# The causal mask of the diagonal score blocks: from two small TensorE products to one VectorE addition

## Chip, cores, metric

The kernel runs on one core of a Trainium2 chip. The metric is the time of one execution on the device in microseconds (us); of several runs the median is given.

## What is computed

The input x has 8 sequences of 512 rows of 128 numbers, in float32. Three layers follow one another: half a mixture-of-experts feed-forward of the normalised rows (32 experts of 64 hidden columns, the 6 best taken within 2 of 4 groups, 16 anchors of 32, one shared expert), then causal attention, then the same feed-forward again. The change touches the attention alone:

```
q, k, v = layernorm(x) @ Wq, Wk, Wv            # 16 heads of 64
scores  = q k^T / 8 + (0 where key <= query, else -inf)
attn    = softmax(scores)                       # over the keys
x       = x + layernorm(x) + (attn v) @ Wo
```

## The kernel before

All engines are programmed by hand. Each has one list of instructions that it works off in order, and semaphores tie the lists together: `pe.wait_ge(s["q_lo"], n + 1)` holds everything that follows it on that engine until VectorE has counted q_lo up to n + 1. There is no scheduler.

The rows are in chunks of 512, one sequence each, so the attention has 8 batches b. Each has 8 slots p, one for a pair of heads, 64 slots in all; n = 8b + p numbers the pairs. float32 products are made of three float32r products, of a high and a low part of each operand: ScalarE takes the high part out of PSUM (`part_hi`: k_hi, q_hi), VectorE the rest (`part_lo`: k_lo, q_lo).

A slot is a software pipeline over four pairs. TensorE's list for slot n (`attn_slot`, L572) is, in this order:

1. `probT` of pair n-1, group 1: 16 transposes of probabilities into PSUM. Its wait, `second_ready`, asks for pT_dve 2n-1, which is VectorE's copy of group 0 of pair n-1, the last copy in the slot before.
2. `scores` of pair n+1, unit 0 (query block 3, 512 keys), then unit 1 (query block 2, 384 keys). In unit 1 the function `third_ready` waits, just ahead of the last products, for the two copies of group 1.
3. `probT` of pair n-1, group 2, then the k projection of pair n+2, a v projection, the output projection of pair n-2, and the q projection of pair n+2, which shares its bank with k and so waits for k_lo.
4. `scores` of pair n+1, unit 2 (query blocks 1 and 0, 256 columns of two banks each), which waits for the exponentials of unit 0 to free the banks.
5. `probT` of pair n, group 0 (16 transposes), then `attend` of pair n-1, 16 products, which wait for q_lo.

A unit writes both heads of the pair, i = 0 and 1, into two PSUM banks. Its real products are L517. After them come four products at L527, which add the mask to the diagonal block: the identity times the mask, both in bf16, in two halves of 64 rows (k = 0, 1), once for each head. They cover 128 columns of each head in units 0 and 1, and 256 in unit 2. Their operands lie in the tile `half`, loaded as float32 and cast by VectorE at L1231 in the first chunk of the first feed-forward.

VectorE's list for a slot (`attn_slot`, L1308) is: copy of group 1 of pair n-1 (`pT_copy`), reciprocal of the row sums (`row_rec`), `row_max` of units 0 and 1 of pair n+1, k_lo, q_lo, `row_max` of unit 2 (two reductions), copy of group 0 of pair n. Some slots have more: p = 1 and 2 normalise rows of the next batch, p = 2 adds the output of the batch before and takes statistics, p = 3 ends these, p = 4 (batches 0 to 6) makes the low part of the next batch's rows ahead of k_lo and has its k projection after the v projection; two slots at the end of batch 6 and the start of batch 7 are shaped like p = 4 for the second feed-forward. Batch 7 carries pieces of routing.

ScalarE's list is: context copy of pair n-2 (`ctx_copy`), its halves of groups 1 and 2, k_hi, the two exponentials of unit 0 (`exp`), the copy of v, q_hi, the two exponentials of unit 1, the four of unit 2. In the slots p = 1 of batches 1 to 7 it also copies the output ahead of q_hi. GpSimd multiplies the probabilities with the reciprocals.

Of the kernel before, what the change touches and what calls it, by code (L numbers as in the profile page):

```python
# [31 lines left out]
P = 128  # L32
# [25 lines left out]
def constants():  # L58

    ident = np.eye(P, dtype=np.float32)  # L60
    mask = np.where(np.arange(P)[None, :] > np.arange(P)[:, None], NEG, 0.0)
    halves = [np.tile(m[i * DK:(i + 1) * DK], (2, 1)) for m in (ident, mask) for i in (0, 1)]
    halves = halves[0:2] + [halves[2], halves[2], halves[3], halves[3]]
    iota = np.broadcast_to(np.arange(E, dtype=np.float32)[None, :], (P, E))
    tie = np.broadcast_to((np.arange(G)[None, :] < np.arange(G)[:, None]), (P, TB, G, G))
    small = np.concatenate([ident, iota, tie.reshape(P, -1), *halves], 1)
    return small.astype(np.float32)


def build(nc, x_in, wg_in, wu_in, wd_in, gate_in, bias_in, wq_in, wk_in, wv_in, wo_in,  # L70
# [6 lines left out]
    with ctx:  # L77
        def sb(name, shape, dt=F32):
            return ctx.enter_context(nc.sbuf_tensor(name, shape, dt))
# [6 lines left out]
        def sem(name):  # L86
# [4 lines left out]
        ident = small[:, 0:P]  # L91
        iota = small[:, P:P + E]
        tie = small[:, P + E:].rearrange("p (t a b) -> p t a b", t=TB, a=G)
        half = sb("half", [P, 6 * P], BF16)
        gate_w = sb("gate_w", [P, E])
        bias = sb("bias", [P, E])
        wg = [sb(f"wg_{n}", [P, HC], F32R) for n in ("hi", "lo")]
# [13 lines left out]
        NZ = 5  # L111
        z = [work[:, i * CH:(i + 1) * CH] for i in range(5, 5 + NZ)]
        spread = work[:, 10 * CH:].rearrange("p (k c) -> p k c", k=NSPREAD)
        half_f32 = work[:, 5 * CH:5 * CH + 6 * P]
        prob = work[:, 0:4 * PW].rearrange("p (r i c) -> p r i c", r=2, i=2)
        values = [work[:, 10 * CH:].rearrange("p (t d) -> p t d", t=TB),
                  sb("values", [P, TB, CH])[:, :, :]]
# [52 lines left out]
        psT, psA, psO = pairs[2], bank[6], bank[7]  # L170


        names = """small_loaded gate_loaded half_loaded half_ready attn_w_loaded
            stat_dve stat_act stat_rows stat_bn rsqrt
            xn_ready xT_ps xT_sb logits_ps sigmoid_done route cwT_ps cwT_sb xT_hi xT_lo
            one_plus gate_up_ps cw_stored silu_done gated_done z_done z_hi z_lo down_ps
            y_evac yT_ps x_added
            aw_hi aw_lo
            a_xn a_xT_ps a_xT_hi a_xT_lo a_xres
            q_ps k_ps v_ps q_hi q_lo k_hi k_lo v_sb s_ps max_done exp_done rec_done norm_done  # L180
            pT_ps pT_act pT_dve ctx_ps ctx_sb out_ps outT_sb outT_ps out_added stored""".split()
        s = {n: sem("s_" + n) for n in names}
        x_loads = [sem(f"s_x_load{c}") for c in range(NC)]
# [72 lines left out]
        def ahead(b, p, d):  # L256

            return b + (p + d) // HP, (p + d) % HP
# [31 lines left out]
        def _(sp):  # L290
# [17 lines left out]
            sp.dma_start(bias[:, :], bias_in.partition_broadcast(P)).then_inc(s["gate_loaded"], 16)  # L308
            load_group(sp, 0)
            load_x(sp, 1)  # L310
            sp.dma_start(half_f32, small_in[:, SMALL:]).then_inc(s["half_loaded"], 16)
            load_group(sp, 1)
            load_down(sp, 0)
            load_down(sp, 1)
            for c in range(2, NC):
                load_x(sp, c)
            for k in range(2, W_GROUPS):
# [53 lines left out]
        def _(pe):  # L371
# [131 lines left out]
            def scores(b, p, u, first, transposes_ready=None):  # L503

                n = pair(b, p)
                if u == 0:
                    pe.wait_ge(s["q_lo"], n + 1)
                    pe.wait_ge(s["k_lo"], n + 1)
                if not (first and p == 0 and u < 2):
                    pe.wait_ge(s["exp_done"], 3 * n + (-1, 0, 1)[u])  # L510
                ps = score_banks(p, u)
                blocks = ([(3, 0, CH)], [(2, 0, 3 * P)], [(1, 0, 2 * P), (0, 2 * P, 2 * P)])[u]
                for qb, o, w in blocks:
                    for k, (a, c) in enumerate(((0, 0), (0, 1), (1, 0))):
                        for i in (0, 1):
                            r = slice(i * DK, (i + 1) * DK)
                            pe.matmul(ps[:, i, o:o + w], qk[0][a][r, p % 2, qb * P:(qb + 1) * P],  # L517
                                      qk[1][c][r, p % 2, 0:w], start=qb != 0 and k == 0, stop=False,
                                      skip_group_check=True)

                o, w = ((3 * P, P), (2 * P, P), (P, 2 * P))[u]
                for k in (0, 1):
                    if k == 1 and transposes_ready is not None:
                        transposes_ready()
                    for i in (0, 1):
                        r = slice(i * DK, (i + 1) * DK)
                        m = pe.matmul(ps[:, i, o:o + w], half[r, k * P:(k + 1) * P],  # L527
                                      half[r, 2 * (k + 1) * P:2 * (k + 1) * P + w], start=False,
                                      stop=k == 1, skip_group_check=True)
                m.then_inc(s["s_ps"], 1)  # L530

            def probT(b, p, g):
# [405 lines left out]
        def _(dve):  # L938
# [240 lines left out]
            def ffn_chunk(g, g0, first, last):  # L1179
# [6 lines left out]
                for j in range(HT):  # L1186
                    if j == 0 and not last and not after_attention:
                        dve.wait_ge(s["xT_ps"], g + 1)
                        normalise(g + 1 - g0, "xn_ready")
                    if setup and j >= 3:  # L1190
                        dve.wait_ge(s["z_done"], tiles(g, j - 3))
                    dve.wait_ge(s["silu_done"], tiles(g, j))
                    if j < HT - 1:
                        tt(gated[j % 3], psU[j % 3], silu[j % 2], ALU.mult) \  # L1194
                            .then_inc(s["gated_done"], 1)
                    else:
                        tt(gated[j % 3][MI:, :], psG[j % 3][MI:, :], silu[j % 2][MI:, :], ALU.mult) \
                            .then_inc(s["gated_done"], 1)
                    if j == 9 and not first:
                        add_y(g - 1, g0)  # L1200
                    if j == XT + 3 and not last:
                        xT_low(g + 1)
                    if j in ROUTING and not last:
                        ROUTING[j](g + 1)
                    if after_attention and j == 18:
                        rows_stats(NC - 1)
                    if after_attention and j == 19:
                        rows_mean(NC - 1, 3 * NC - 1)
                    if j == at_stats and measure:
                        dve.wait_ge(s["x_added"], g)  # L1210
                        rows_stats(g - 1)
                    if j == at_mean and measure:
                        rows_mean(g - 1, middle_stats(g - 1))
                    if g < NC - 2 and j == at_input_stats:
                        dve.wait_ge(x_loads[g + 2], 16)
                        rows_stats(g + 2)
                    if g < NC - 2 and j == at_input_stats + 1:
                        rows_mean(g + 2, input_stats(g + 2))
                    if 0 < g < NC - 2 and j == 18:
                        finish_std(g + 2)  # L1220
                    if before_attention and j == 15:
                        finish_std(STD_MIDDLE)
                    if before_attention and j == 16:
                        a_rows(0, True, range(TB))
                    if before_attention and j == 17:
                        a_residual(0)
                    if setup and j == 2:
                        split_lo(1, 0)
                        split_lo(1, 1)
                        dve.wait_ge(s["half_loaded"], 16)  # L1230
                        nc.vector.tensor_copy(half[:, :], half_f32).then_inc(s["half_ready"], 1)  # L1231
                        dve.wait_ge(s["half_ready"], 1)
                    for k in range(setup_scaled(j - 1), setup_scaled(j)) if setup else (j,):
                        scale(g, k, first)
                if setup:
# [30 lines left out]
            def part_lo(b, p, which, early, special=False):  # L1266
# [9 lines left out]
                else:  # L1276
                    tt(lo, ps, f32(hi), ALU.subtract).then_inc(s["k_lo"], 1)

            def row_max(b, p, u):
                n = pair(b, p)  # L1280
                dve.wait_ge(s["s_ps"], 3 * n + u + 1)
                ps = score_banks(p, u)
                for qb, o in (((3, 0),), ((2, 0),), ((1, 0), (0, 2 * P)))[u]:
                    m = nc.vector.tensor_reduce(nmax[:, p % 2, :, qb], ps[:, :, o:o + (qb + 1) * P],  # L1284
# [23 lines left out]
            def attn_slot(b, p, first, last):  # L1308
# [6 lines left out]
                if p == 2 and not first:  # L1315
                    add_out(b - 1)
                if have_s:
                    row_max(*ahead(b, p, 1), 0)
                    row_max(*ahead(b, p, 1), 1)
                if next_rows(b, p):  # L1320
                    a_xT_low(b + 1, psA)
                if ffn_rows(b, p):
                    xT_low(NC)
                if have_q:
                    part_lo(*ahead(b, p, 2), 1, False, special_slot(b, p))
                if p == 2 and not first:
                    dve.wait_ge(s["out_added"], b)
                    rows_stats(b - 1)
                if p == 3 and not first:
                    rows_mean(b - 1, b - 1 + 2 * NC)  # L1330
                if have_q:
                    part_lo(*ahead(b, p, 2), 0, False)
                if have_s:
                    row_max(*ahead(b, p, 1), 2)
                if pair(b, p) == NC * HP - 1:
                    route_onehot(NC)
# [22 lines left out]
                        piece(NC)  # L1359

            def attention():
                row_max(0, 0, 0)
                row_max(0, 0, 1)
                add_y(NC - 1, 0)
                part_lo(0, 1, 1, True)
                row_max(0, 0, 2)
                part_lo(0, 1, 0, True)
                for p in range(HP):
# [117 lines left out]
```

## Time and profile before

| | |
|---|---|
| median of 3 runs | 1465.37 us (1463.87 to 1465.82) |
| the profiled execution | 1465.29 us, its span 1463.5 us |
| TensorE busy | 1426.8 us, 97% |
| VectorE busy | 1081.9 us, 74% |
| ScalarE busy | 805.5 us, 55% |
| GpSimd busy | 286.3 us, 20% |
| first feed-forward | about 0 to 418 us of the span |
| attention | about 418 to 1054 us |
| second feed-forward | to the end |

The span is the time from the first instruction to the last on the chip. Busy time counts instructions that overlap once. An engine that is busy for 97% of the span leaves little for others to wait on, but a product that is counted as busy may still stream slower than it could, and the share is an average over three stages.

### The profile page before, as it was taken

Reading aid. Unit: us, or ns where it says so; the run is one execution under the profiler, and the core shown is the slowest. Engines: PE = TensorE matmul, PEld = TensorE weight load, DVE = VectorE, ACT = ScalarE, POOL = GpSimd, SP = SyncE. Lnnn points to the kernel's source line nnn. Section 1 sums busy time; section 2 is a strip of 40 time slices with the busy share of each in tenths; the row PEclk is TensorE's granted clock in tenths of the full one; section 3 lists DMA queues with packets and bytes.
Section 4 is the critical chain, followed back from the end, with each engine's and each line's share of the span. In section 5 each row is a group of like instructions: output and inputs, shape, how many; then the busy total and the mean of one; then the engine's idle time right before and its main releaser. Section 6 shows DMA issues by size and latency. Waiting matters only on the chain.

```text
span 1463.5 us, 27264 instructions
## 1 busy us (share of the span) xinstructions
PE 1426.8 (97%) x9616; PEld 951.9 (65%) x9616; DVE 1081.9 (74%) x2451; ACT 805.5 (55%) x1911; POOL 286.3 (20%) x585
## 2 busy tenths in 40 slices
PE   5999999999979999999999999999899999999998
PEld 4666666666656666666666666666566666666665
DVE  8888888888667676776767677767767877787775
ACT  4344344433457777777787777777644233323332
POOL 1000000000214344344444434434400000000000
PEclk9999999999999999999999999999999999999999
DMA  6543333333300000000000000000033433333332
GB/s 229 161 131 110 111 102 117 106 116 98 114 22 2 1 2 2 2 2 2 1 2 2 2 2 2 2 2 2 2 110 108 121 116 113 110 119 121 111 118 86
DMA packets 59024, 98.06 MB, mean 67 GB/s; under 512 B 6160, under 2 KB 15504, under 8 KB 58896
## 3 DMA queue, kind: packets, MB, share of 16 engines
q1 hardware_dynamic: 58896, 96.38, 21.1%
q8 instruction: 77, 1.26, 0.4%
q14 instruction: 51, 0.42, 0.1%
HBM read 92.68 MB, written 3.67 MB: 66 GB/s over the span
## 4 chain that ended last, share of the span: by engine, by line
PE 90%; DVE 4%; ACT 3%; issue 1%; POOL 0%; DMA 0%; SPq 0%; POOLq 0%; ACTq 0%; DVEq 0%
PE banks L416 19%; PE banks L199 14%; PE banks L201 13%; PE banks L200 13%; PE banks L552 10%; PE banks L517 9%; PE banks L538 6%; PE banks L565 3%; PE banks L527 2%; PE banks L375 2%; ACT work L843 1%; PE banks L387 1%; DVE q_lo L1273 1%; DVE work L1194 1%; POOL work L1428 0%
## 5 line engine op out<-in xcount | busy, mean ns | idle before, releaser
L787 ACT ACTIVATE work<-banks 128x512 f32<-128x512 f32 x320 | 190.9, 597 | 444.8 <-PE banks L201 440.8
L416 PE MATMUL banks<-work,wd 128*128 128x512 f32 x672 | 342.1, 592 | 0.3 <-DVE work L1168 0.2
L1194 DVE TENSOR_TENSOR work<-banks,work 128x512 f32<-128x512 f32 x320 | 220.8, 690 | 145.7 <-ACT work L787 141.3
L843 ACT ACTIVATE work<-banks,nmax 128x512 f32<-128x512 f32 (+3 forms) x512 | 263.7, 527 | 39.1 <-DVE nmax L1284 39.1
L1428 POOL TENSOR_SCALAR work<-work,rrec 128x512 f32<-128x512 f32 (+3 forms) x512 | 262.7, 542 | 0.0
L199 PE MATMUL banks<-xT_hi,wg_hi 128*128 128x512 f32 x336 | 248.4, 739 | 0.7 <-DVE wu_lo L1159 0.6
L1168 DVE TENSOR_TENSOR work<-work 128x512 f32<-128x512 f32 x320 | 225.3, 704 | 7.4 <-DMA work<-cw_rows 3.3
L1284 DVE TENSOR_REDUCE nmax<-banks 128x2 f32<-128x1024 f32 (+3 forms) x256 | 198.9, 818 | 9.9 <-PE banks L527 5.5
L1299 DVE COPY stage<-banks 128x1024 f32<-128x1024 f32 (+1 forms) x128 | 122.0, 953 | 59.0 <-PE banks L538 58.8
L416 PEld LDWEIGHTS banks<-work,wd 128*128 128x128 f32 x672 | 126.5, 189 | 33.7 <-issue 2.4
L201 PE MATMUL banks<-xT_hi,wg_lo 128*128 128x512 f32 x336 | 133.7, 398 | 0.0
L200 PE MATMUL banks<-xT_lo,wg_hi 128*128 128x512 f32 x336 | 133.5, 397 | 0.0
L199 PE MATMUL banks<-xT_hi,wu_hi 128*128 128x512 f32 x320 | 127.2, 397 | 0.0
L200 PE MATMUL banks<-xT_lo,wu_hi 128*128 128x512 f32 x320 | 127.1, 397 | 0.0
L201 PE MATMUL banks<-xT_hi,wu_lo 128*128 128x512 f32 x320 | 127.0, 397 | 0.0
L854 ACT ACTIVATE stage<-banks 128x512 f32<-128x512 f32 x128 | 76.5, 598 | 86.7 <-PE banks L538 84.6
L538 PE MATMUL banks<-small,work 64*128 64x64 f32 x2560 | 114.6, 225 | 4.3 <-DVE stage L1299 2.7
L538 PEld LDWEIGHTS banks<-small,work 64*128 64x128 f32 x2560 | 98.2, 138 | 17.6 <-issue 16.0
L1273 DVE SCALAR_TENSOR_TENSOR q_lo<-banks,q_hi 128x512 fp32r<-128x512 f32 x64 | 44.3, 692 | 87.0 <-ACT q_hi L821 87.0
L199 PEld LDWEIGHTS banks<-xT_hi,wg_hi 128*128 128x128 f32 x336 | 64.3, 191 | 67.9 <-issue 65.3
L200 PEld LDWEIGHTS banks<-xT_lo,wg_hi 128*128 128x128 f32 x336 | 64.4, 192 | 65.6 <-issue 65.3
L843 ACT ACTIVATION_READ_ACCUMULATOR work<-banks,nmax 128x1 f32 x512 | 105.4, 206 | 0.0
(135 smaller groups left out, 2191.6 us busy)
## 6 DMA issues: line engine op xcount, KB each, us to landing
work<-cw_rows SPq DMA_DIRECT2D x320, 256.0 KB, 3.1
x<-in_x SPq DMA_DIRECT2D x8, 256.0 KB, 6.6
out_rows<-x SPq DMA_DIRECT2D x8, 256.0 KB, 2.2
cw_rows<-cwT SPq DMA_DIRECT2D x16, 96.0 KB, 1.9
stage<-in_w_gate SPq DMA_DIRECT2D x3, 448.0 KB, 4.9
wd<-in_w_down SPq DMA_DIRECT2D x3, 448.0 KB, 7.7
stage<-in_w_up SPq DMA_DIRECT2D x2, 448.0 KB, 6.5
stage<-in_wq SPq DMA_DIRECT2D x1, 512.0 KB, 4.0
```

The lines of the kernel that those rows point to most:

```text
L199: pe.matmul(o, w[0], m[0], start=start, stop=False, skip_group_check=True)
L200: pe.matmul(o, w[0], m[1], start=False, stop=False, skip_group_check=True)
L201: return pe.matmul(o, w[1], m[0], start=False, stop=stop, skip_group_check=True)
L416: pe.matmul(psY, wd[:, j * P:(j + 1) * P], z[part_slot(j)], start=j == 0, stop=j == HT - 1, skip_group_check=True).then_inc(s["down_ps"], 1)
L538: m = pe.transpose(psT[:, h, k * DK:(k + 1) * DK], prob[r, p % 2, i, o:o + P], ident[r, h * DK:(h + 1) * DK])
L552: m = pe.matmul(psA[i * DK:(i + 1) * DK, kb * P:], values[p // TB][:, kb, p % TB * P + i * DK:p % TB * P + (i + 1) * DK], pT[:, p % 2, o:o ...
L787: nc.scalar.activation(silu[j % 2], psG[j % 3], ACT.Silu) \
L843: m = nc.scalar.activation(prob[:, p % 2, i, o:o + w], ps[:, i, so:so + w], ACT.Exp, bias=nmax[:, p % 2, i, qb:qb + 1], accum_out=rsum[:, ...
L1168: tt(z[part_slot(j)], gated[j % 3], spread[:, j % NSPREAD, :], ALU.mult) \
L1194: tt(gated[j % 3], psU[j % 3], silu[j % 2], ALU.mult) \
L1284: m = nc.vector.tensor_reduce(nmax[:, p % 2, :, qb], ps[:, :, o:o + (qb + 1) * P], AX.X, ALU.max, negate=True)
L1428: nc.gpsimd.tensor_scalar(t, t, rrec[:, par, i, qb:qb + 1], 1.0, ALU.mult, ALU.mult) \
```

## The change

VectorE gets the mask as a float32 tile of 128 x 128 and adds it in PSUM, in place, to the diagonal block of each unit, for both heads in one instruction, and the row maximum waits for that. An instruction covers 256 elements in each partition in units 0 and 1, and 512 in unit 2. TensorE's four bf16 products of each unit go. The wait that stood between them (`transposes_ready`) now stands ahead of the last pair of the real products. On VectorE the row maximum of unit 1 moves behind k_lo; the addition of unit 1 stays where that maximum was. The load of 384 KB of bf16 operands as float32, with its cast, goes, and a load of 64 KB takes its place, two issues later on the same queue.

```diff
-        half = sb("half", [P, 6 * P], BF16)
+        mask = sb("mask", [P, P])
@@ SyncE
-            sp.dma_start(half_f32, small_in[:, SMALL:]).then_inc(s["half_loaded"], 16)
             load_group(sp, 1)
             load_down(sp, 0)
             load_down(sp, 1)
+            sp.dma_start(mask[:, :], small_in[:, SMALL:]).then_inc(s["mask_loaded"], 16)
@@ TensorE, scores()
                 for qb, o, w in blocks:
+                    final = qb in (3, 2, 0)
                     for k, (a, c) in enumerate(((0, 0), (0, 1), (1, 0))):
+                        if k == 2 and final and transposes_ready is not None:
+                            transposes_ready()
                         for i in (0, 1):
                             r = slice(i * DK, (i + 1) * DK)
-                            pe.matmul(ps[:, i, o:o + w], qk[0][a][r, p % 2, qb * P:(qb + 1) * P],
-                                      qk[1][c][r, p % 2, 0:w], start=qb != 0 and k == 0, stop=False,
-                                      skip_group_check=True)
-
-                o, w = ((3 * P, P), (2 * P, P), (P, 2 * P))[u]
-                for k in (0, 1):
-                    if k == 1 and transposes_ready is not None:
-                        transposes_ready()
-                    for i in (0, 1):
-                        r = slice(i * DK, (i + 1) * DK)
-                        m = pe.matmul(ps[:, i, o:o + w], half[r, k * P:(k + 1) * P],
-                                      half[r, 2 * (k + 1) * P:2 * (k + 1) * P + w], start=False,
-                                      stop=k == 1, skip_group_check=True)
+                            m = pe.matmul(ps[:, i, o:o + w], qk[0][a][r, p % 2, qb * P:(qb + 1) * P],
+                                          qk[1][c][r, p % 2, 0:w], start=qb != 0 and k == 0,
+                                          stop=final and k == 2, skip_group_check=True)
                 m.then_inc(s["s_ps"], 1)
@@ VectorE, first chunk
-                        dve.wait_ge(s["half_loaded"], 16)
-                        nc.vector.tensor_copy(half[:, :], half_f32).then_inc(s["half_ready"], 1)
-                        dve.wait_ge(s["half_ready"], 1)
@@ VectorE, attention
+            def mask_scores(b, p, u):
+                n = pair(b, p)
+                dve.wait_ge(s["s_ps"], 3 * n + u + 1)
+                if n == 0 and u == 0:
+                    dve.wait_ge(s["mask_loaded"], 16)
+                o, w = ((3 * P, P), (2 * P, P), (P, 2 * P))[u]
+                ps = score_banks(p, u)[:, :, o:o + w].rearrange("p i (b c) -> p i b c", c=P)
+                tt(ps, ps, mask[:, :].unsqueeze(1).unsqueeze(1).broadcast_to([P, 2, w // P, P]), ALU.add) \
+                    .then_inc(s["masked"], 1)
             def row_max(b, p, u):
-                dve.wait_ge(s["s_ps"], 3 * n + u + 1)
+                dve.wait_ge(s["masked"], 3 * n + u + 1)
@@ attn_slot of VectorE
+                    mask_scores(*ahead(b, p, 1), 0)
                     row_max(*ahead(b, p, 1), 0)
-                    row_max(*ahead(b, p, 1), 1)
+                    mask_scores(*ahead(b, p, 1), 1)
 ...
                 if have_q:
                     part_lo(*ahead(b, p, 2), 1, False, special_slot(b, p))
+                if have_s:
+                    row_max(*ahead(b, p, 1), 1)
 ...
                     part_lo(*ahead(b, p, 2), 0, False)
                 if have_s:
+                    mask_scores(*ahead(b, p, 1), 2)
                     row_max(*ahead(b, p, 1), 2)
```

## Rows read from the trace of the kernel before

**Rows 1.** The page: busy time of each engine.

```profile
PE 1426.8 (97%) x9616; PEld 951.9 (65%) x9616; DVE 1081.9 (74%) x2451; ACT 805.5 (55%) x1911; POOL 286.3 (20%) x585
```

**Rows 2.** The page: the chain that ended last, share of the span by line.

```profile
PE banks L416 19%; PE banks L199 14%; PE banks L201 13%; PE banks L200 13%; PE banks L552 10%; PE banks L517 9%; PE banks L538 6%; PE banks L565 3%; PE banks L527 2%; PE banks L375 2%; ACT work L843 1%; PE banks L387 1%; DVE q_lo L1273 1%; 
```

**Rows 3.** The chain in order of time, one slot: start us, us, what.

```profile
668.64 0.64 PE banks L538 x16
669.28 0.75 PE banks L517 x6
670.16 0.58 PE banks L517 x6
670.87 0.25 PE banks L538 x8
...
675.29 0.23 PE banks L527 x4
...
678.33 0.64 PE banks L538 x16
```

**Rows 4.** Timeline, that slot, VectorE: start us, us, instruction, idle before.

```profile
669.33 0.69 DVE L1299 COPY stage<-banks 128x512 f32<-128x512 f32 x1 [1.20 <-PE banks L538]
670.20 2.09 DVE L1284 TENSOR_REDUCE nmax<-banks 128x2 f32<-128x1024 f32 x2
672.67 0.69 DVE L1277 TENSOR_TENSOR k_lo<-banks,k_hi 128x512 fp32r<-128x512 f32 x1 [0.38 <-ACT k_hi L821]
675.05 0.69 DVE L1273 SCALAR_TENSOR_TENSOR q_lo<-banks,q_hi 128x512 fp32r<-128x512 f32 x1 [1.69 <-ACT q_hi L821]
675.66 1.01 DVE L1284 TENSOR_REDUCE nmax<-banks 128x2 f32<-128x512 f32 x2
676.59 1.21 DVE L1299 COPY stage<-banks 128x1024 f32<-128x1024 f32 x1
```

**Rows 5.** Timeline, that slot, TensorE and ScalarE.

```profile
673.42 0.19 PEld L199 LDWEIGHTS banks<-xT_hi,aw_hi 128*128 128x128 f32 x1 [0.62 <-DVE k_lo L1277]
674.42 0.60 ACT L821 ACTIVATE q_hi<-banks 128x512 fp32r<-128x512 f32 x1
675.95 2.38 PE L552 MATMUL banks<-stage,values 128*64 128x512 f32 x16
676.71 0.47 ACT L843 ACTIVATE work<-banks,nmax 128x256 f32<-128x256 f32 x1 [0.57 <-DVE nmax L1284]
678.26 0.71 PE L538 MATMUL banks<-small,work 64*128 64x64 f32 x16
678.38 0.60 ACT L865 ACTIVATE ctx_sum<-banks 128x512 f32<-128x512 f32 x1
```

**Rows 6.** Groups by line and shape, 420 to 1020 us: busy, mean ns, idle.

```profile
L1284 DVE TENSOR_REDUCE nmax<-banks 128x2 f32<-128x512 f32 x60 | 40.9, 682 | 0.0
L1284 DVE TENSOR_REDUCE nmax<-banks 128x2 f32<-128x256 f32 x60 | 25.0, 417 | 0.0
```

**Rows 7.** Timeline, routing of the first chunk, VectorE.

```profile
14.74 0.18 DVE L1034 TENSOR_TENSOR t<-t 128x32 f32<-128x32 f32 x1
14.85 0.18 DVE L1035 TENSOR_TENSOR t<-t 128x32 f32<-128x32 f32 x1
15.06 0.19 DVE L1037 TENSOR_TENSOR t<-t,t 128x32 f32<-128x32 f32 x1
```

**Rows 8.** Timeline, slots p = 1 and p = 4 of one batch, VectorE.

```profile
685.18 0.69 DVE L1273 SCALAR_TENSOR_TENSOR q_lo<-banks,q_hi 128x512 fp32r<-128x512 f32 x1 [2.11 <-ACT q_hi L821]
...
714.34 0.69 DVE L1277 TENSOR_TENSOR k_lo<-banks,k_hi 128x512 fp32r<-128x512 f32 x1 [1.62 <-ACT k_hi L821]
715.35 0.69 DVE L1273 SCALAR_TENSOR_TENSOR q_lo<-banks,q_hi 128x512 fp32r<-128x512 f32 x1 [0.31 <-ACT q_hi L821]
```

**Rows 9.** Timeline, VectorE behind the cast, and at the first scores.

```profile
29.79 0.69 DVE L1168 TENSOR_TENSOR work<-work 128x512 f32<-128x512 f32 x1 [0.23 <-DMA work<-cw_rows]
...
418.07 2.09 DVE L1284 TENSOR_REDUCE nmax<-banks 128x2 f32<-128x1024 f32 x2 [1.19 <-PE banks L527]
```

More of the change, by code:

```diff
@@ L61, in constants @@
     mask = np.where(np.arange(P)[None, :] > np.arange(P)[:, None], NEG, 0.0)
-    halves = [np.tile(m[i * DK:(i + 1) * DK], (2, 1)) for m in (ident, mask) for i in (0, 1)]
-    halves = halves[0:2] + [halves[2], halves[2], halves[3], halves[3]]
     iota = np.broadcast_to(np.arange(E, dtype=np.float32)[None, :], (P, E))
     tie = np.broadcast_to((np.arange(G)[None, :] < np.arange(G)[:, None]), (P, TB, G, G))
-    small = np.concatenate([ident, iota, tie.reshape(P, -1), *halves], 1)
+    small = np.concatenate([ident, iota, tie.reshape(P, -1), mask], 1)
     return small.astype(np.float32)
@@ L113, in build @@
         spread = work[:, 10 * CH:].rearrange("p (k c) -> p k c", k=NSPREAD)
-        half_f32 = work[:, 5 * CH:5 * CH + 6 * P]
         prob = work[:, 0:4 * PW].rearrange("p (r i c) -> p r i c", r=2, i=2)
@@ L170, in build @@
         psT, psA, psO = pairs[2], bank[6], bank[7]
-        names = """small_loaded gate_loaded half_loaded half_ready attn_w_loaded
+        names = """small_loaded gate_loaded mask_loaded attn_w_loaded
             stat_dve stat_act stat_rows stat_bn rsqrt
@@ L179, in build @@
             a_xn a_xT_ps a_xT_hi a_xT_lo a_xres
-            q_ps k_ps v_ps q_hi q_lo k_hi k_lo v_sb s_ps max_done exp_done rec_done norm_done
+            q_ps k_ps v_ps q_hi q_lo k_hi k_lo v_sb s_ps masked max_done exp_done rec_done norm_done
             pT_ps pT_act pT_dve ctx_ps ctx_sb out_ps outT_sb outT_ps out_added stored""".split()
@@ L1361, in attention @@
             def attention():
+                mask_scores(0, 0, 0)
                 row_max(0, 0, 0)
+                mask_scores(0, 0, 1)
                 row_max(0, 0, 1)
@@ L1365, in attention @@
                 part_lo(0, 1, 1, True)
+                mask_scores(0, 0, 2)
                 row_max(0, 0, 2)
```

## The prediction

> **What bounds the kernel now.** I read the page first. TensorE is busy 97% of the span and VectorE 74% [rows 1], and the chain that ended last is TensorE almost throughout, with the mask products at 2% [rows 2]. So the first reading is: the products that go are on the chain, and VectorE has time for the additions. Shares don't settle it, though, so I then laid one ordinary slot out in order of time, once by the chain [rows 3] and once with all engines [rows 4, 5]. The reader is to see three things there.
>
> First, the slot lasts 678.33 - 668.64 = 9.69 us, and TensorE streams through it. In the list of the chain the mask products of units 0 and 1 are gaps: 669.28 + 0.75 = 670.03 to 670.16 is 0.13 us, 670.16 + 0.58 = 670.74 to 670.87 is again 0.13, and unit 2's are a row of their own, 0.23 [rows 3]. Together 0.49 us a slot, 64 x 0.49 = 31 us of the span, which is the 2% of [rows 2].
>
> Second, VectorE's idle time lies where it waits for others: 1.20 us ahead of the copy of group 1, 0.38 ahead of k_lo, 1.69 ahead of q_lo, 3.3 us in 9.69. Behind q_lo it has none until the slot is over: q_lo at 675.05, row maxima of unit 2 at 675.66, copy of group 0 from 676.59 to 677.80 [rows 4].
>
> Third, TensorE's next slot begins at 678.26 [rows 5] with transposes that overwrite what this copy reads (`second_ready`). From VectorE's end to TensorE's start such a wait takes 673.42 - (672.67 + 0.69) = 0.06 us [rows 4, 5]. The copy would have let TensorE start at 677.80 + 0.06 = 677.86. The slack of this second chain is 0.40 us, and it is what the change spends.
>
> **The change part by part.** I count from T, the start of a slot's first transposes: T = 678.26 - 9.69 = 668.57.
>
> *TensorE, units 0 and 1.* The products that go save 0.13 + 0.13. A part of these gaps may be a pause between kinds of product that stays in another form; a pair of 512 columns takes 0.23, so four of 128 should stream in half that, 0.12. I take 0.25 for the two units, bounds 0.2 and 0.26. Everything down to q_hi follows TensorE, provided that VectorE's part above is hidden, which I check next: q_hi starts at T + 5.85 [rows 5] and would start at T + 5.60.
>
> *VectorE, units 0 and 1.* The trace has no addition that writes PSUM. The nearest rows are the subtraction of 512 elements from PSUM and SBUF, 0.69 us [rows 4], and reductions of 512 and 256 elements, 0.68 and 0.42 [rows 6]. I take 0.42 and 0.69; nothing of that kind is below the 0.42, and a write into PSUM could cost some 0.1 more. The addition is followed by a wait of the engine for its own result. Three small operations show what that costs: without a wait the next starts 14.85 - 14.74 = 0.11 after the last, with one 15.06 - 14.85 = 0.21, for the same 0.18 of duration [rows 7]. So a waiting successor starts at duration plus 0.03, a free one at duration less 0.08. Addition 0 can start when unit 0 is through, at about T + 1.5; the maximum of unit 0 follows at 1.95 to 3.18, addition 1 at 3.1 to 3.5. k_lo before stands at T + 4.10 and must move to T + 3.85, since the q projection starts right at its end; VectorE is free 0.3 us earlier. The moved maximum of unit 1, with 0.95 us, fits the idle 1.69 between k_lo and q_lo. Cost of these: nothing, covered by VectorE's own idle time. Without that cover it would be 0.42 for each addition.
>
> *VectorE, unit 2.* Here nothing covers. q_lo at T + 6.48 moves to T + 6.23 and its successor to T + 6.84. Before, that was the maximum of unit 2; now it is the addition of 512 elements, and the maximum comes 0.69 + 0.03 = 0.72 later. The scores themselves are ready in time, so the 0.23 that TensorE saves in unit 2 is worth nothing. The copy of group 0 ends at 677.80 - 668.57 = T + 9.23, less 0.25, plus 0.72: T + 9.70, and TensorE may go on at T + 9.76. Before it went on at T + 9.69. **An ordinary slot thus becomes 0.07 us longer**, where a slot bound by TensorE alone would be 0.49 shorter. Bounds: 0.2 saved and an addition 0.1 dearer give +0.22; a wait that costs nothing gives -0.04.
>
> *The rule.* The skill weighs the wait otherwise. The Trainium skill, VectorE: DVE Perf Modes, section The DRAIN you can't avoid, says that chained operations cost the same with a semaphore after each as with one at the end, and advises to keep the number of operations down, not the semaphores. By that the maximum would come 0.61 behind the addition, and the slot would be 0.04 shorter than before; the rows above speak against it, with 0.21 against 0.11. Its other half, fewer operations, speaks against the change.
>
> *TensorE's moved wait.* In unit 1 `third_ready` now stands ahead of the last real pair, about 0.1 us earlier within the unit. It asks for ScalarE's copy of group 1, which stands behind the exponentials of unit 2 and the context copy. These start 0.04 us behind the maximum [rows 4, 5], now at T + 8.6; the context copy follows 678.38 - 676.71 = 1.67 us later at the most, about T' + 0.5 with T' the next slot's start, and the copy of group 1 ends at about T' + 1.6. The loading of weights behind the wait stood at T' + 1.55. It is just met: 0 to 0.1 us.
>
> *Slots with more in them.* p = 1, seven of them: ScalarE holds q_hi back, VectorE idles 2.11 us and q_lo is at 685.18 [rows 8], so TensorE waits for q_lo and sets the end of the slot some 0.6 us later than the copy would; the 0.25 is kept: 7 x -0.25 = -1.8. p = 4, seven, and two like it: k_lo comes at 714.34 and q_lo 1.01 behind it [rows 8]. The moved maximum must fit between: k_lo, 0.61, maximum, 0.87, q_lo is 1.48, so q_lo is 0.47 late, on top of the 0.07: 9 x 0.54 = +4.9. p = 2, seven: addition of the output ahead of unit 0 and statistics between k_lo and q_lo take up the cover; I take 0.2 each, +1.4, bounds 0.07 and 0.5. The remaining 64 - 23 = 41 slots x 0.07 = +2.9. In the first two slots and ahead of them TensorE already waits for VectorE: the first maximum idles until TensorE's unit 0 is through [rows 9], so an addition of 0.45 less 0.13 is on the path there, and one of 0.72 twice; I take +1.5. The end of batch 7, with routing behind the copy of group 0, I take as +0.5.
>
> *Loads.* The cast goes, but VectorE idles 0.23 us for a load right behind it [rows 9], so the next multiplication stays where it is: 0. The mask is needed 380 us later: 0. The feed-forwards are unchanged.
>
> Sum: -1.8 + 4.9 + 1.4 + 2.9 + 1.5 + 0.5 = +9.4. The profiled execution took 1465.29 us and becomes 1474.7; the median before is 0.1 higher, so I say **1474.7 us**.
>
> **The rivals.**
>
> *A: TensorE stays the bound (faster).* If TensorE can start its slot when its own work is done, the change gives 64 x -0.49 = -31: 1434 us. For it: 97% against 74%. Against it: the copy of group 0 would have to end by T + 9.14, 0.56 earlier than I find. It decides where addition and wait together take below 0.16 us in unit 2, or where the copy is not what releases the transposes. A mixture, with half of this, would be 1450.
>
> *B: the wait is free.* If the successor starts 0.61 behind the addition (this is what the rule above claims), 0.11 less in 57 slots is -6: 1468.5, slower by 0.2%, at the edge of what can be measured; with the full 0.26 saved, 1467. Against it: 0.21 against 0.11 in [rows 7].
>
> *C: ScalarE's late copy catches TensorE, or PSUM is dear.* If `third_ready` is met 0.15 to 0.2 us late, or the addition of unit 2 costs that much more than a subtraction that writes SBUF, 57 x 0.17 = +10: 1485. For it: 0.05 us of margin in my own reckoning. Against it: the wait holds a weight load that runs ahead of its product by about as much.
>
> **How the numbers follow.** About 0.2%, 3 us, is what a measurement of this kernel tells from no change. My forecast has a chance of 0.52, its own range 1468.5 to 1481; A 0.14; B 0.12; C 0.17; something else, 0.05, half to each side. The range leaves out A, the far end of C and the like, and keeps B and half of the unknown: 1460 to 1487. Faster than 1462.4: A and the half, with the lowest part of B, 0.18. Within 3 us: most of B and the low edge of the forecast, 0.12. Slower: 0.70.
>
> **What would show it.** The chain that ended last should no longer run on TensorE alone in ordinary slots: q_lo, the addition of unit 2, the maxima, the copy L1299, then the transposes L538, with TensorE idle about 0.5 us ahead of these. The additions should read 0.42 and 0.69 us, the maximum of unit 2 should start 0.72 behind the addition, and a slot should last 9.76. In p = 4 q_lo should be late behind the moved maximum. VectorE's idle time ahead of q_lo should fall from 1.69 to about 0.8. VectorE's busy time should rise by 64 x (0.42 + 0.42 + 0.69) = 98 us. Wrong would be: no wait of TensorE for L1299 (A); a wait of TensorE for the copy of ScalarE in unit 1 (C); a granted clock below the present one, which I don't price.

## The result and the profile after

The changed kernel takes 1481.49 us (median of 4 runs, 1481.23 to 1483.76), the kernel before, on the same chip, 1465.59. The ratio is 1.0111, with a 95% interval of 1.0096 to 1.0126: 14 to 18.5 us slower. The profiled execution has a span of 1479.9 us, 16.4 more than before. All of it arises in the attention: VectorE's last copy of group 1 starts at 1078.65 us, before at 1062.27.

The page's busy times and the chain that ended last, as in [rows 1] and [rows 2]:

```profile
PE 1404.6 (95%) x8848; PEld 947.1 (64%) x8848; DVE 1170.0 (79%) x2642; ACT 798.3 (54%) x1911; POOL 286.1 (19%) x585
...
PE 65%; DVE 17%; ACT 10%; issue 7%; POOL 0%; DMA 0%; SPq 0%; DVEq 0%; POOLq 0%; ACTq 0%
PE banks L413 19%; PE banks L196 12%; PE banks L198 11%; PE banks L197 11%; PE banks L517 5%; ACT work L833 5%; DVE stage L1296 4%; PE banks L528 4%; DVE nmax L1281 3%; DVE q_lo L1260 3%; DVE banks L1273 3%; ACT q_hi L811 2%; PE banks L372 
```

TensorE has 768 products and 22 us of busy time less, VectorE 88 us more, and the chain now passes through VectorE's q_lo (L1260), the addition (L1273), the maxima (L1281) and the copy (L1296). ScalarE's share of it is 10%, where it was 3%: in an ordinary slot the chain goes from k_hi through ScalarE's list (the exponentials of unit 0, the copy of v) to q_hi, and from there to q_lo. In the groups of the window 420 to 1020 us the row of the transposes names the new wait, 28.4 us for the copy L1296; before, all 2360 of them in the same window had idled 1.9 us. The rows, first TensorE, then the additions of both shapes:

```profile
L528 PE MATMUL banks<-small,work 64*128 64x64 f32 x2296 | 103.5, 224 | 28.4 <-DVE stage L1296 28.4
L1273 DVE TENSOR_TENSOR banks<-banks,mask 128x256 f32<-128x256 f32 x117 | 49.9, 427 | 3.4 <-PE banks L517 3.4
L1273 DVE TENSOR_TENSOR banks<-banks,mask 128x512 f32<-128x512 f32 x59 | 40.7, 690 | 0.0
```

One ordinary slot in the timeline, with the rows that answer to [rows 4] and [rows 5]. T, the start of the first transposes (the loading of their weights), is 666.90 here:

```profile
666.90 0.60 PEld L528 LDWEIGHTS banks<-small,work 64*128 64x128 f32 x16 [0.72 <-issue]
667.29 0.61 ACT L855 ACTIVATE ctx_sum<-banks 128x512 f32<-128x512 f32 x1
667.76 0.62 ACT L844 ACTIVATE stage<-banks 128x512 f32<-128x512 f32 x1
668.43 0.43 DVE L1273 TENSOR_TENSOR banks<-banks,mask 128x256 f32<-128x256 f32 x1
668.50 0.22 PEld L517 LDWEIGHTS banks<-k_hi,q_lo 64*128 64x128 f32 x2
668.78 0.44 PE L528 MATMUL banks<-small,work 64*128 64x64 f32 x8
668.90 1.23 DVE L1281 TENSOR_REDUCE nmax<-banks 128x2 f32<-128x1024 f32 x1
670.04 0.42 DVE L1273 TENSOR_TENSOR banks<-banks,mask 128x256 f32<-128x256 f32 x1
670.77 0.69 DVE L1264 TENSOR_TENSOR k_lo<-banks,k_hi 128x512 fp32r<-128x512 f32 x1 [0.31 <-ACT k_hi L811]
671.38 0.95 DVE L1281 TENSOR_REDUCE nmax<-banks 128x2 f32<-128x768 f32 x1
671.52 0.19 PEld L196 LDWEIGHTS banks<-xT_hi,aw_hi 128*128 128x128 f32 x1 [0.63 <-DVE k_lo L1264]
672.52 0.60 ACT L811 ACTIVATE q_hi<-banks 128x512 fp32r<-128x512 f32 x1
673.15 0.69 DVE L1260 SCALAR_TENSOR_TENSOR q_lo<-banks,q_hi 128x512 fp32r<-128x512 f32 x1 [0.82 <-ACT q_hi L811]
673.76 0.69 DVE L1273 TENSOR_TENSOR banks<-banks,mask 128x512 f32<-128x512 f32 x1
674.49 1.02 DVE L1281 TENSOR_REDUCE nmax<-banks 128x2 f32<-128x512 f32 x2
675.42 1.22 DVE L1296 COPY stage<-banks 128x1024 f32<-128x1024 f32 x1
676.75 0.61 PEld L528 LDWEIGHTS banks<-small,work 64*128 64x128 f32 x16 [0.72 <-issue]
676.78 0.68 PE L528 MATMUL banks<-small,work 64*128 64x64 f32 x15 [0.51 <-DVE stage L1296]
```

The slot lasts 676.75 - 666.90 = 9.85 us, against 9.69 before. The reader is to see that VectorE runs from 673.15 to 676.64 without a pause, and that TensorE waits 0.51 us for the last of these operations while it has nothing else to do. Above q_lo VectorE still has pauses: the additions of units 0 and 1 delay nobody.

### The profile page after: what moved, and what is told of

Same layout as the page of the kernel before. It is cut to its first block, busy times and chain, and to the rows that moved or that the text cites. A ratio compares the mean times of both kernels' runs of the same rounds, so it can differ in the third digit from the quotient of the medians.

```text
span 1479.9 us, 25920 instructions
## 1 busy us (share of the span) xinstructions
PE 1404.6 (95%) x8848; PEld 947.1 (64%) x8848; DVE 1170.0 (79%) x2642; ACT 798.3 (54%) x1911; POOL 286.1 (19%) x585
## 4 chain that ended last, share of the span: by engine, by line
PE 65%; DVE 17%; ACT 10%; issue 7%; POOL 0%; DMA 0%; SPq 0%; DVEq 0%; POOLq 0%; ACTq 0%
PE banks L413 19%; PE banks L196 12%; PE banks L198 11%; PE banks L197 11%; PE banks L517 5%; ACT work L833 5%; DVE stage L1296 4%; PE banks L528 4%; DVE nmax L1281 3%; DVE q_lo L1260 3%; DVE banks L1273 3%; ACT q_hi L811 2%; PE banks L372 2%; PE banks L542 1%; ACT work L819 1%
## 5 line engine op out<-in xcount | busy, mean ns | idle before, releaser
L1281 DVE TENSOR_REDUCE nmax<-banks 128x2 f32<-128x1024 f32 (+3 forms) x256 | 204.7, 821 | 4.5
L1296 DVE COPY stage<-banks 128x1024 f32<-128x1024 f32 (+1 forms) x128 | 122.0, 953 | 37.7 <-PE banks L528 37.5
L528 PEld LDWEIGHTS banks<-small,work 64*128 64x128 f32 x2560 | 106.7, 138 | 48.0 <-issue 46.9
L1273 DVE TENSOR_TENSOR banks<-banks,mask 128x256 f32<-128x256 f32 (+1 forms) x192 | 98.7, 514 | 5.7 <-PE banks L517 5.7
```

The source lines that it names most:

```text
L528: m = pe.transpose(psT[:, h, k * DK:(k + 1) * DK], prob[r, p % 2, i, o:o + P], ident[r, h * DK:(h + 1) * DK])
L1296: nc.vector.tensor_copy(*transposed(p, g, slice(0, 2 - g))).then_inc(s["pT_dve"], 1)
```

## The experiments

T-numbers below are us behind the slot's first transposes. The length of a slot is read from the starts of VectorE's copy of group 1 in successive slots.

**Unit 2's mask back on TensorE.** The changed kernel, with the four bf16 products for unit 2 alone. The excerpt does not show the rest: their operands are loaded and cast again, VectorE adds nothing in unit 2, and its maximum waits for TensorE.

```diff
-                    final = qb in (3, 2, 0)
+                    final = qb in (3, 2, 0) and u not in (2,)
 ...
+                if u in (2,):
+                    o, w = ((3 * P, P), (2 * P, P), (P, 2 * P))[u]
+                    for k in (0, 1):
+                        if k == 1 and transposes_ready is not None:
+                            transposes_ready()
+                        for i in (0, 1):
+                            r = slice(i * DK, (i + 1) * DK)
+                            m = pe.matmul(ps[:, i, o:o + w], half[r, k * P:(k + 1) * P],
+                                          half[r, 2 * (k + 1) * P:2 * (k + 1) * P + w], start=False,
+                                          stop=k == 1, skip_group_check=True)
```

> Units 0 and 1 get the mask from VectorE as in the changed kernel, unit 2 from TensorE's bf16 products as before. My theory: only the addition of unit 2 lies on the chain (q_lo, addition, maxima, copy of group 0, next transposes), the additions of units 0 and 1 are hidden. Then TensorE sets an ordinary slot again and it lasts 9.69 - 0.25 = 9.44 us; with p = 1 at -0.25 and p = 4 at about +0.1 (moved maximum ahead of q_lo) the time is about 12 us below before: 1453 us. Rival, VectorE as a whole is too full and each addition costs alike: the slot stays near 9.69 or above, 1466 to 1476 us.

Measured: 1452.65 us, ratio to before 0.9906 (0.9891 to 0.9921). An ordinary slot lasts 9.38 us. Its timeline, VectorE and TensorE:

```profile
658.88 0.69 DVE L1282 TENSOR_TENSOR k_lo<-banks,k_hi 128x512 fp32r<-128x512 f32 x1 [0.26 <-ACT k_hi L826]
...
661.87 1.01 DVE L1304 TENSOR_REDUCE nmax<-banks 128x2 f32<-128x512 f32 x2
662.15 2.37 PE L557 MATMUL banks<-stage,values 128*64 128x512 f32 x16
662.79 1.22 DVE L1319 COPY stage<-banks 128x1024 f32<-128x1024 f32 x1
664.46 0.71 PE L543 MATMUL banks<-small,work 64*128 64x64 f32 x16
```

The copy ends at 664.01 and TensorE takes its transposes at 664.46, when its own products are through: it is the bound again. Two additions a slot, 64 x 2 x 0.43 = 55 us of VectorE's time, cost nothing; taking them in place of TensorE's products gains 13 us. The rival, that each addition costs alike, is out.

**Only unit 2 on VectorE.** The complement: the products of units 0 and 1 stay, with the load and the cast, and the maximum of unit 1 stays in its old place.

```diff
-                    final = qb in (3, 2, 0)
+                    final = qb in (3, 2, 0) and u not in (0, 1)
 ...
+                if u in (0, 1):            # the four products, as above
 ...
             def mask_scores(b, p, u):
+                if u not in (2,):
+                    return
```

> The kernel before with one part of the change alone: unit 2 gets the mask from VectorE, units 0 and 1 from TensorE, the maximum of unit 1 stays in its old place. My theory: nothing is saved ahead of q_hi, and all of addition and wait, 0.73 us, goes onto the chain against a slack of 0.35 to 0.40: an ordinary slot lasts about 10.08 us, 57 slots x 0.39 = +22: 1487 us, so more than the whole change. Rival, each addition costs alike: a third of the change's +16, 1471 us.

Measured: 1493.0 us, ratio 1.0186 (1.0171 to 1.0202). The slot lasts 10.13 us:

```profile
661.31 0.69 DVE L1319 COPY stage<-banks 128x512 f32<-128x512 f32 x1 [0.89 <-PE banks L543]
...
667.06 0.69 DVE L1278 SCALAR_TENSOR_TENSOR q_lo<-banks,q_hi 128x512 fp32r<-128x512 f32 x1 [1.69 <-ACT q_hi L826]
667.67 0.69 DVE L1293 TENSOR_TENSOR banks<-banks,mask 128x512 f32<-128x512 f32 x1
668.39 1.02 DVE L1304 TENSOR_REDUCE nmax<-banks 128x2 f32<-128x512 f32 x2
669.33 1.21 DVE L1319 COPY stage<-banks 128x1024 f32<-128x1024 f32 x1
671.44 0.69 DVE L1319 COPY stage<-banks 128x512 f32<-128x512 f32 x1 [0.89 <-PE banks L543]
```

One third of the change costs more than all of it, and more than the 1487 us expected: the slot is 0.43 us longer where 0.39 was reckoned, and 4.6 us are lost in the first slots of batch 0, which the expectation did not price. The two parts have opposite signs: -13 us and +27 us, with sum +14, near the whole change's +16. VectorE's idle 1.69 ahead of q_lo is as long as before and helps nothing.

**No mask in unit 2.** The changed kernel, leaving out the mask of query blocks 1 and 0; all bf16 products are gone, as in the change.

```diff
             def mask_scores(b, p, u):
+                if u not in (0, 1):
+                    return
```

> The changed kernel, leaving out the mask of unit 2 (query blocks 0 and 1 see later keys of their own block). My theory: the chain through VectorE ends at T + 9.74 - 0.73 + 0.11 = 9.12, TensorE's own work at 9.69 - 0.49 = 9.20, so an ordinary slot lasts 9.2 us and all that TensorE saves comes out: about -23 us, 1442 us. Rival, something else than the addition of unit 2 holds the slots (ScalarE's late copy, the maximum of unit 1): at or above 1460 us.

Measured: 1444.9 us, ratio 0.9856 (0.9841 to 0.9871), 37 us below the changed kernel for one instruction a slot less, and its wait. An ordinary slot lasts 9.23 us. In its timeline q_lo ends at 658.69 and the first weights of `attend` are loaded 0.06 us later, after waiting for it:

```profile
658.00 0.69 DVE L1260 SCALAR_TENSOR_TENSOR q_lo<-banks,q_hi 128x512 fp32r<-128x512 f32 x1 [0.82 <-ACT q_hi L811]
658.08 0.66 PE L528 MATMUL banks<-small,work 64*128 64x64 f32 x16
...
658.75 0.20 PEld L542 LDWEIGHTS banks<-stage,values 128*64 128x64 f32 x4 [0.15 <-DVE q_lo L1260]
```

So even with that addition at no cost, unit 2's products would be worth only 9.38 - 9.23 = 0.15 of their 0.23 us, since q_lo is next in line.

**The addition of unit 2 in two.** Each maximum waits for its own addition only, so the first one has an instruction between itself and what it reads.

```diff
-                ps = score_banks(p, u)[:, :, o:o + w].rearrange("p i (b c) -> p i b c", c=P)
-                tt(ps, ps, mask[:, :].unsqueeze(1).unsqueeze(1).broadcast_to([P, 2, w // P, P]), ALU.add) \
-                    .then_inc(s["masked"], 1)
+                for o in ((3 * P,), (2 * P,), (P, 2 * P))[u]:
+                    ps = score_banks(p, u)[:, :, o:o + P]
+                    tt(ps, ps, mask[:, :].unsqueeze(1).broadcast_to([P, 2, P]), ALU.add) \
+                        .then_inc(s["masked"], 1)
 ...
+                    dve.wait_ge(s["masked"], 4 * n + u + h + 1)     # ahead of each maximum
```

> The changed kernel, the addition of unit 2 as two of 256 elements, each maximum waiting for its own one only. If a wait of VectorE for its own last result costs the 0.12 us that I took, the first maximum starts 0.34 + 0.34 = 0.68 behind the first addition, not 0.73, and the slot is 0.05 us shorter: -3 us against the changed kernel, 1478 us. If waits are free, the additional instruction only costs: 0.68 against 0.61, +4 us, 1485 us. If what costs is mainly the number of instructions, also 1485 us.

Measured: 1477.34 us, ratio 1.008 (1.0066 to 1.0094), against 1.0111 (1.0096 to 1.0126) of the changed kernel. The slot lasts 9.77 us, 0.08 less. The timeline:

```profile
662.18 0.69 DVE L1260 SCALAR_TENSOR_TENSOR q_lo<-banks,q_hi 128x512 fp32r<-128x512 f32 x1 [0.81 <-ACT q_hi L811]
662.79 0.75 DVE L1273 TENSOR_TENSOR banks<-banks,mask 128x256 f32<-128x256 f32 x2
663.45 1.01 DVE L1281 TENSOR_REDUCE nmax<-banks 128x2 f32<-128x512 f32 x2
```

The maxima start 0.66 behind the first addition, where one addition of the same 512 elements took 674.49 - 673.76 = 0.73. One instruction more is cheaper here than one wait for the engine's own last result. The two intervals lie just apart, and the slot lengths show the same sign and size: 57 x 0.08 = 4.6 us.

The changed kernel has the same comparison within one slot p = 2. There VectorE is late, so that k_lo follows the addition of unit 1 without a wait for it:

```profile
1025.45 0.42 DVE L1273 TENSOR_TENSOR banks<-banks,mask 128x256 f32<-128x256 f32 x1
1025.79 0.68 DVE L1264 TENSOR_TENSOR k_lo<-banks,k_hi 128x512 fp32r<-128x512 f32 x1
```

It starts 0.34 us behind the addition's start (0.33 or 0.34 in all seven such slots), where the maximum of unit 0, which waits for its addition, starts 668.90 - 668.43 = 0.47 behind it.

**The maximum of unit 1 back in the nine slots with a late k projection.**

```diff
                     mask_scores(*ahead(b, p, 1), 1)
+                    if special_slot(b, p):
+                        row_max(*ahead(b, p, 1), 1)
 ...
-                if have_s:
+                if have_s and not special_slot(b, p):
                     row_max(*ahead(b, p, 1), 1)
```

> The changed kernel with the maximum of unit 1 back in its old place in the nine slots that have their k projection late (p = 4 of batches 0 to 6 and two like it), and only there. My theory: there the moved maximum stands between k_lo and q_lo, which are only 1.0 us apart, and makes q_lo 0.47 us late: 9 x 0.47 = -4 us against the changed kernel, about 1477 us; p = 4 falls from 10.96 to about 10.5 us. Rival, q_lo has room there: no difference.

Measured: 1478.6 us, ratio 1.0082 (1.0068 to 1.0096). The interval touches that of the changed kernel, so the gain rests on the slots: p = 4 lasts 10.49 us, in the changed kernel 10.95. First that slot in the changed kernel, then here:

```profile
722.60 0.69 DVE L1264 TENSOR_TENSOR k_lo<-banks,k_hi 128x512 fp32r<-128x512 f32 x1 [1.62 <-ACT k_hi L811]
723.21 0.95 DVE L1281 TENSOR_REDUCE nmax<-banks 128x2 f32<-128x768 f32 x1
724.08 0.68 DVE L1260 SCALAR_TENSOR_TENSOR q_lo<-banks,q_hi 128x512 fp32r<-128x512 f32 x1
```

```profile
719.67 0.96 DVE L1281 TENSOR_REDUCE nmax<-banks 128x2 f32<-128x768 f32 x1
...
721.96 0.69 DVE L1264 TENSOR_TENSOR k_lo<-banks,k_hi 128x512 fp32r<-128x512 f32 x1 [0.73 <-ACT k_hi L811]
722.97 0.69 DVE L1260 SCALAR_TENSOR_TENSOR q_lo<-banks,q_hi 128x512 fp32r<-128x512 f32 x1 [0.32 <-ACT q_hi L811]
```

The distance from k_lo to q_lo falls from 1.48 to 1.01 us, what it was in [rows 8]: the 0.47 of the forecast. The seven slots p = 4 gain 3.2 us together, and the two like them, of 11.44 and 11.31 us, another 1.3.

**The maximum of unit 1 back in all slots.** The same edit without the condition.

> The changed kernel with the maximum of unit 1 back in its old place in all slots. My theory: it ends at about T + 4.4, k_lo starts at T + 4.4 rather than at 3.87, the q projection and all behind it are 0.45 to 0.5 us late: an ordinary slot lasts about 10.3 us, +22 for 46 slots, -4 for the nine: 1499 us. Rival, the place of this maximum doesn't matter: 1481 us.

Measured: 1506.9 us, ratio 1.0281 (1.0265 to 1.0296). The ordinary slot lasts 10.43 us. k_lo follows the maximum without a pause and starts at T + 4.47 (T is 665.70 here), where the changed kernel has T + 3.87:

```profile
668.84 0.42 DVE L1273 TENSOR_TENSOR banks<-banks,mask 128x256 f32<-128x256 f32 x1
669.29 0.96 DVE L1281 TENSOR_REDUCE nmax<-banks 128x2 f32<-128x768 f32 x1
670.17 0.68 DVE L1264 TENSOR_TENSOR k_lo<-banks,k_hi 128x512 fp32r<-128x512 f32 x1
```

The 0.60 that k_lo is late comes back as 0.58 of the slot. So the additions of units 0 and 1 are free only because the maximum was moved with them: the cover is what VectorE idles ahead of k_lo in the changed kernel, 0.31 us. The time is 8 us above the 1499 expected. The ordinary slot was put 0.13 too short, and the seven slots p = 2 last 10.95 us in place of 9.95, 7 us together, for which nothing had been reckoned.

**Both findings together.** Unit 2's mask on TensorE, and the maximum of unit 1 early in the nine slots.

> Unit 2's mask on TensorE, units 0 and 1 on VectorE, and the maximum of unit 1 in its old place in the nine slots with the late k projection. My theory: as the run with unit 2 on TensorE, 1452.7 us, less up to 9 x 0.3 = 2.7 us (that slot lasted 9.68 us there, against 9.38 of an ordinary one): 1450 us, faster than the kernel before by 1%. Rival, those slots are held by TensorE's own extra work, 0.60 us: 1452.7 us.

Measured: 1448.05 us (1447.41 to 1449.08), ratio 0.9879 (0.9864 to 0.9894): 18 us faster than the kernel before and 33 us faster than the changed one. The slot p = 4 lasts 10.03 us, with 10.31 without this last edit (the expectation's 9.68 is not its length by the copies of group 1), and the nine slots together are 3.0 us shorter, where 2.7 was expected. What the last edit does to the whole time is not clear of noise: the intervals of this run and of the one with unit 2 on TensorE overlap.

## Why the prediction was right, point by point

The direction, the mechanism and its place were as forecast: slower, because the addition of unit 2 and the wait behind it outgrow the 0.40 us of slack of VectorE's second chain. The three runs that take the parts of the change by themselves show it. The measured time lies in the upper half of the range, 0.5 us above the likeliest case's own range; the shift was 16 us where the forecast had 9. The size was thus too small by 7 us, and nearly every term that missed missed to the same side.

*TensorE's saving ahead of q_hi.* Forecast 0.25; q_hi started at T + 5.62 instead of 5.85, so 0.23. In the run with unit 2 on TensorE k_lo stands at T + 3.80 instead of 4.10: 0.30 is there to be had. The changed kernel loses 0.07 of it at the moved wait of unit 1, behind which the weights of the second transposes are loaded at T + 1.73 here and at T + 1.66 there (T is 655.08 there). First the changed kernel, then that run:

```profile
668.63 0.45 PEld L528 LDWEIGHTS banks<-small,work 64*128 64x128 f32 x8
```

```profile
656.74 0.44 PEld L543 LDWEIGHTS banks<-small,work 64*128 64x128 f32 x8
```

ScalarE's context copy, which stands ahead of the copy that this wait asks for, is at T + 0.39 here and T + 0.12 there, and the last pair of unit 1 takes 397 ns here in the mean and 344 there. This is the mechanism of rival C, at a small size and within the 0 to 0.1 of the forecast. It is read from timelines and was not tried by itself.

*Additions.* Forecast 0.42 and 0.69, measured 0.427 and 0.690. An addition that reads and writes PSUM costs what the subtraction into SBUF costs, so the dear branch of C is out. These additions alone read 98.7 us, forecast 98; VectorE's busy time, which counts overlaps once, rose by 88. Its idle time ahead of q_lo fell to 0.82, forecast 0.8. The maximum starts 0.73 behind the addition, forecast 0.72.

*The rule on semaphores.* The Trainium skill, VectorE: DVE Perf Modes, section The DRAIN you can't avoid, has the semaphores within a chain of copies as free. Rival B was built on the same claim, and for these operations it is refuted: 0.73 with the wait, against 0.61 for the free successor of q_lo (673.15 to 673.76), 0.47 against 0.34 behind an addition of 256 elements, and the run with two additions got faster by putting an instruction in the place of the wait. So the advice on the number of operations, which that page gives under Rules for kernel authors, did not hold for this pair either.

*End of the chain.* The copy ends at T + 9.74, forecast 9.70. From there the loading of weights starts after 0.11 us, where I had taken 0.06 from k_lo. Slot 9.85 against 9.76; 0.16 longer than before and not 0.07. The right price stood in the trace of the kernel before, in the one slot in which TensorE did wait for this copy:

```profile
437.02 1.21 DVE L1299 COPY stage<-banks 128x1024 f32<-128x1024 f32 x1
438.35 0.60 PEld L538 LDWEIGHTS banks<-small,work 64*128 64x128 f32 x16 [2.03 <-issue]
```

438.35 - (437.02 + 1.21) = 0.12 us: a wait is best priced from a row of the same kind, even if there is only one.

*The sum by its terms*, from the copies of group 1 in both traces. The first term that was mis-sized is the ordinary slot: 34 of them (without the first four and the last three) cost 34 x 0.16 = 5.4, forecast 2.4. The seven p = 1 came out at 10.19 to 10.31 instead of 10.51 to 10.57, together -1.9 (forecast -1.8). The seven p = 2 at 9.95 instead of 9.70, +1.7 (forecast 1.4). The seven p = 4 at 10.95 instead of 10.33, +4.3 (forecast 3.8, of which 0.47 each was shown by putting the maximum back). The two like them are not alike: 11.44 and 11.31 instead of 10.40 and 10.52, +1.8 where the forecast had 1.1. The last slots gave +0.6, forecast 0.5 and three times 0.07.

The second mis-sized term is the beginning: when the slot p = 4 of batch 0 starts, the changed kernel is 4.35 us behind, copy of group 1 at 476.01 against 471.66, where I had +1.5 and four slots of 0.07. The runs show what carries it. The same copy stands at 471.56 without unit 2's mask, at 472.87 with unit 2's mask on TensorE, and at 476.22 with only unit 2's on VectorE: it is the addition of unit 2 again, in slots where VectorE's list was on the chain already. Single executions scatter here, though: the run with the maximum early in nine slots has the code of the changed kernel up to this point and reads 476.67, and the two runs with unit 2 on TensorE, again alike up to here, read 472.87 and 471.15. The granted clock of TensorE in these stretches was 0.94 before and 0.91 after. How much of the 4.35 it makes is open. The sum of all these terms is the 16.4 of the span.

*Rival A* (faster by 31 us, TensorE as the bound) fails on the copy of group 0, as said. The run without unit 2's mask shows how near it was: there the slot is 9.23, near its 9.20.

*The loads and the cast* cost and gave nothing: the first addition starts at 418.02, where the first maximum had started at 418.07 [rows 9].

## What to carry to other kernels

Ask of an idle engine not how much it idles, but on which side of its own critical result the idle time lies: here 3.3 us of idle time took two additions for nothing, once a maximum had been moved out of their way, and 0.40 us of slack was all that the third had. A change that consists of several like parts may be a gain and a loss at once, so price each at its place and keep those that are covered; here two of three parts made the kernel 1% faster, and all three made it 1% slower. If an operation has to go into a tight chain, try to put other work of the same engine between it and its first reader; here that gave back 0.08 us a slot.

## What was not expected of the hardware

The release of TensorE's transposes by VectorE's copy took 0.11 or 0.12 us in nearly all slots of the changed kernel, where that of a projection by k_lo takes 671.52 - (670.77 + 0.69) = 0.06 in the same slot; why the one takes twice the other is open. The wait of VectorE for its own last result, 0.12 us (0.73 against 0.61), had been expected from three small operations; that it outweighs a further instruction, 0.66 against 0.73 for the same 512 elements, is what a count of operations would not have told.
